# A four-layer graph kernel: the second graph layer's first map made with features on the partitions

## The reference

```python
H = (adj != 0)                       # 1024 x 1024 incidence
w = adj[:, 0, :]                     # first row: weight of each hyperedge
Dn = 1 / einsum('nce,ne->nc', H, w)  # node degree (0 where the sum is 0)
Be = 1 / H.sum(axis=1)               # edge degree
def conv(x, W, b):
    return Dn[:, :, None] * (H @ (Be[:, :, None] * (H.T @ (x @ W.T)))) + b
h = relu(conv(x, W1, b1))            # 256 -> 512 features
h = layer_norm(h, gamma, beta)
y = conv(h, W2, b2)                  # 512 -> 256 features
return y + x
```

## Time and profile before

| | |
|---|---|
| median of 3 runs | 2956.13 us (2955.24 to 2957.43) |
| profiled execution, its own time | 2953.71 us |
| its span, first to last instruction | 2951.9 us |
| PE busy | 2919.8 us (99%) |
| DVE busy | 1871.9 us (63%) |
| ACT busy | 1477.3 us (50%) |
| POOL busy | 719.8 us (24%) |
| mean granted TensorE clock | 0.999 of full speed |

### The profile page before, as it was taken

How to read it: one execution, slowest core, us unless ns; L and a number is a source line. 1 busy time by engine, 2 the same in 40 slices (tenths; PEclk the granted TensorE clock), 3 DMA queues, 4 the chain that set the end, 5 groups by cost and what they waited for, 6 DMA issues and landing times.

```text
span 2951.9 us, 63497 instructions
## 1 busy us (share of the span) xinstructions
PE 2919.8 (99%) x23040; PEld 2374.1 (80%) x23040; DVE 1871.9 (63%) x4154; ACT 1477.3 (50%) x2761; POOL 719.8 (24%) x1305
## 2 busy tenths in 40 slices
PE   8999999999999999999999999999999999999999
PEld 7888788887888878888688886888868888688886
DVE  3797427874288742887428864388643986439862
ACT  2883317833288332883228732387323872238622
POOL 0342003420034201342013420134101341014410
PEclk9999999999999999999999999999999999999999
DMA  5202212023120230211311112112122021220200
GB/s 177 94 2 93 93 58 94 4 92 111 47 87 24 71 135 33 78 51 52 129 51 59 60 59 113 70 40 70 65 97 79 31 86 67 79 79 30 84 8 15
DMA packets 95318, 204.29 MB, mean 69 GB/s; under 512 B 10513, under 2 KB 41617, under 8 KB 94993
## 3 DMA queue, kind: packets, MB, share of 16 engines
q1 hardware_dynamic: 93456, 195.76, 18.3%
q0 software_dynamic: 1536, 4.20, 0.4%
HBM read 136.75 MB, written 8.65 MB: 49 GB/s over the span
## 4 chain that ended last, share of the span: by engine, by line
PE 83%; DVE 12%; ACT 3%; issue 2%; DMA 0%; SPq 0%; DVEq 0%; ACTq 0%
PE ps L1133 39%; PE ps L1319 15%; PE ps L1297 8%; PE ps L1348 8%; PE ps L1410 7%; PE ps L1485 4%; DVE junk L843 3%; DVE stats L640 1%; DVE h L859 1%; DVE dn L852 1%; DVE h L877 1%; PE ps L1173 1%; DVE shiftB L874 1%; ACT Uh L1100 1%; DVE Ul L685 1%
## 5 line engine op out<-in xcount | busy, mean ns | idle before, releaser
L801 DVE CUSTOM_DVE_ANT_0 Z<-ps,adjN 128x1024 f32<-128x1024 f32 x512 | 623.6, 1218 | 54.0 <-PE ps L1297 45.9
L1057 ACT ACTIVATE Z<-Z,nm 128x1024 f32<-128x1024 f32 x512 | 589.7, 1152 | 5.3 <-POOL nm L577 5.3
L1319 PE MATMUL ps<-ident,Z 128*128 128x128 f32 x4096 | 538.5, 274 | 1.4 <-ACT Z L1057 1.2
L1319 PEld LDWEIGHTS ps<-ident,Z 128*128 128x128 f32 x4096 | 463.2, 140 | 88.6 <-issue 38.0
L1297 PE MATMUL ps<-kS,qS 128*128 128x512 f32 x1024 | 371.9, 445 | 3.3 <-issue 2.3
L589 POOL TENSOR_SCALAR H<-adjN 128x128 fp32r<-128x128 f32 (+1 forms) x456 | 317.5, 696 | 0.0
L577 POOL TENSOR_TENSOR nm<-nm,minus 128x1 f32<-128x1 f32 x512 | 97.1, 190 | 550.1 <-DVE nm L801 549.7
L1133 PE MATMUL ps<-mh,adjT 128*128 128x256 f32 x1024 | 223.6, 379 | 0.8 <-issue 0.8
L1133 PE MATMUL ps<-v,P 128*128 128x257 f32 x1024 | 223.6, 379 | 0.0
L1133 PE MATMUL ps<-hT,t3T 128*128 128x512 f32 x512 | 221.0, 592 | 0.0
L1133 PEld LDWEIGHTS ps<-v,P 128*128 128x128 f32 x1024 | 193.8, 189 | 31.9 <-issue 3.8
(11 more groups left out here) (183 smaller groups left out, 5870.8 us busy)
## 6 DMA issues: line engine op xcount, KB each, us to landing
adjT<-adjT_in SPq DMA_DIRECT2D x8, 4096.0 KB, 13.1
adjN<-adj_in SPq DMA_DIRECT2D x8, 4096.0 KB, 17.5
adjT<-adjT_in SPq DMA_DIRECT2D x8, 2048.0 KB, 11.8
qS<-qhi SPq DMA_DIRECT2D x112, 128.0 KB, 2.1
qS<-qlo SPq DMA_DIRECT2D x112, 128.0 KB, 2.1
adjT<-adjT_in SPq DMA_DIRECT2D x8, 1536.0 KB, 6.5
xn<-x_in SPq DMA_DIRECT2D x8, 1024.0 KB, 5.7
out<-x SPq DMA_DIRECT2D x8, 1024.0 KB, 4.9
```

The source lines that it names most:

```text
L801: dve.tensor_tensor_reduce(Z[:, u % ZS], ps[:, 2 * (u % 2):2 * (u % 2) + 2].rearrange("p a n -> p (a n)"), adjN[:, u // HEADS], SCORE_SCAL ...
L1057: act.activation(Z[:, u % ZS], Z[:, u % ZS], ACT.Exp, bias=nm[:, u:u + 1], accum_out=sm[:, u:u + 1]).then_inc(exps.sem, 1)
L1319: mm = pe.transpose(ps[:, turn_bank((u, s)), rows(a)], Z[:, u % ZS, rows(NT // 2 * s + a)], ident[:])
```

## The change

In layer 2:

- **y** is made with features on the partitions: `W1h` is now the stationary side and `A2T` the moving one, in 8 products of 128 features by 512 nodes. The node degree can't be a per-partition scalar there, so it is multiplied into `A2T` by DVE, as a row on all partitions (`dnB`). That row comes from `dn` by two DMAs: out to DRAM in 1024 pieces of 4 bytes (`dn_kept`), and back to all 128 partitions.
- ACT's relu with the bias as a column writes `h2T` at once; the 32 transposes and 8 copies of `h2T` go.
- The row mean is an additional column of ones in `W2g` (products 257 wide). The mean square comes from DVE: four squares and three additions for each half (`add_squares`), which PE sums over the partitions with a column of ones (`sum_squares`). Mean and variance are formed for two node tiles at a time (`moments`), POOL makes `rstd` for these (four times).
- The node weights are computed earlier, two of the eight tiles at steps 66 and 74 of the attention, four before the first `be`, two between; by another instruction (the one that L801 uses), into two `junk` rows. For that `wB` is loaded early.
- `HT`: DVE makes tiles 0 to 4, spread between other work, POOL makes tiles 5 to 7.
- POOL's additions to `x` wait for the inverted node weights.
- **a3** runs in passes: source tiles 0 to 3 for the outputs of the four free banks first, then for the other four.

```diff
-                sp.wait_ge(*adjT_back[2](b, 16))
-                stand(sp, waited_sp)
-                sp.dma_start(wB[:], adj_in[bass.ds(b, 1)][0, 0].partition_broadcast(P)).then_inc(wB_in.sem, 16)
                 sp.dma_start(W1h[:], w1T.rearrange("(t p) d -> p t d", p=P)).then_inc(w2_in.sem, 16)
...
+                sp.wait_ge(*chain(b, 8))
+                stand(sp, waited_sp)
+                sp.dma_start(dn_kept.rearrange("t p -> p t"), dn[:, 3], allow_slow_non_contiguous=True).then_inc(dn_out.sem, 16)
+                sp.wait_ge(*dn_out(b, 16))
+                stand(sp, waited_sp)
+                sp.dma_start(dnB[:], dn_kept.rearrange("t p -> (t p)").partition_broadcast(P)).then_inc(dnB_in.sem, 16)
...
+                for t in range(HT_DVE, NT):
+                    part = [t in tiles for tiles in BACK].index(True)
+                    pool.wait_ge(*adjT_back[part](b, 16))
+                    stand(pool, waited_pool)
+                    pool.tensor_scalar(HT[:, t], adjT[:, t], 0.0, 0.0, ALU.is_equal, ALU.is_equal).then_inc(HTs_pool.sem, 1)
                 pool.wait_ge(*hhs(b, NT))
                 pool.wait_ge(*hls(b, NT))
-                pool.wait_ge(*HTs(b, NT))
+                pool.wait_ge(*chain(b, 8))
                 pool.tensor_tensor(x[:], x[:], hh[:, :, 0:D].bitcast(F32), ALU.add).then_inc(xh.sem, 1)
...
+                for t in range(2, 6):
+                    node_weights(t)
+                incidence_T(0)
+                for t in range(TPH + 1):
+                    edge_degree(t)
                     if t:
                         lower(Ul, Uh, t - 1, uhs, Us)
...
+                incidence_T(1)
+                node_weights(6)
+                incidence_T(2)
+                node_weights(7)
+                invert_weights()
+                for t in range(TPH, NT):
+                    if t - 1 < HT_DVE:
+                        incidence_T(t - 1)
+                    if t + 1 < NT:
+                        edge_degree(t + 1)
+                    lower(Ul, Uh, t, uhs, Us)
+
+                dve.wait_ge(*dnB_in(b, 16))
+                for n in range(DT * NH):
+                    dve.wait_ge(*a2_ps(b, n + 1))
+                    dve.tensor_tensor(A2T[:, n % DT, half(n // DT)], ps[:, 4 + n], dnB[:, half(n // DT)], ALU.mult).then_inc(a2s.sem, 1)
+
+                def add_squares(s):
+
+                    for f in range(FT):
+                        done = (2 * FT - 1) * s + max(0, 2 * f - 1)
+                        dve.wait_ge(*h2Ts(b, FT * s + f + 1))
+                        if f > 1:
+                            dve.wait_ge(*sq_part(b, done))
+                        dve.tensor_tensor(sq[:, s, min(f, 1)], h2T[:, f, half(s)], h2T[:, f, half(s)], ALU.mult).then_inc(sq_part.sem, 1)
+                        if f:
+                            dve.wait_ge(*sq_part(b, done + 1))
+                            dve.tensor_tensor(sq[:, s, 0], sq[:, s, 0], sq[:, s, 1], ALU.add).then_inc(sq_part.sem, 1)
...
+                add_squares(0)
+                add_squares(1)
...
+                mean_squares(0)
+                moments(0)
+                for t in range(0, NT, 2):
+                    if t:
+                        lower_rows(t - 1)
+                    scale_rows(t)
+                    scale_rows(t + 1)
+                    lower_rows(t)
+                    if t == 0:
+                        mean_squares(1)
+                    if t + 2 < NT:
+                        moments(t // 2 + 1)
+                lower_rows(NT - 1)
...
+                for n in range(FT * NH):
+                    s, f = n // FT, n % FT
+                    act.wait_ge(*y_ps(b, n + 1))
+                    act.activation(h2T[:, f, half(s)], ps[:, n % 4], ACT.Relu, bias=b1c[:, f:f + 1]).then_inc(h2Ts.sem, 1)
...
+                sum_squares(0)
...
                 for t in range(NT):
+                    if t == 2:
+                        sum_squares(1)
...
-                sum_up(*of_edges(Uh, Ul, D), (x2s,), [None] * 4 + [x2t(b, t + 1) for t in range(4, NT)], a3_ps)
+                pe.wait_ge(*mean_sq(b, NH))
+                sum_up(*of_edges(Uh, Ul, D), (x2s,), [None] * 4 + [x2t(b, t + 1) for t in range(4, NT)], a3_ps,
+                       passes=((range(TPH), range(TPH)), (range(TPH), range(TPH, NT)), (range(TPH, NT - 2), range(NT))))
```

More of the change, by code:

```diff
@@ L167, in build_program @@
         _, PTb, rs, Rs = p1b
-        h2, h2T = p2
+        _, h2T = p2
         hh, hl, wB, junk = p2a
+        dnB = wB
         Vh, Vl = p2v
         P3, E3 = p3
-        _, shiftB, b1B = p2c
+        _, shiftB = p2c
         (r1, r2, r3) = region(
             [("v", [P, NT, D], F32)],
-            [("W1h", [P, DT, HID], F32), ("W2g", [P, FT, D], F32)],
+            [("W1h", [P, DT, HID], F32), ("W2g", [P, FT, HW], F32)],
             [("xn", [P, NT, D], F32)],
@@ L867, in batch @@
-                for t in range(NT):
-                    if t % TPH == 0:
-                        dve.wait_ge(*nmrs(b, after(3, t // TPH)))
-                    if t == TPH - 1:
-                        shift(b, 3, 1)
+                incidence_T(1)
[9 more added lines that the diff above has]
+                    lower(Ul, Uh, t, uhs, Us)
@@ L1459, in batch @@
-                for t in range(NT):
-                    if t == H2T_AT:
-                        transpose_h2(0)
-                    if t % TPH == 0:
-                        pe.wait_ge(*a2s(b, DT * (t // TPH + 1)))
-                    if t >= 4:
-                        pe.wait_ge(*ys(b, t - 3))
-                    product(ps[:, t % 4], [(A2T[:, c, rows(t)], W1h[:, c]) for c in range(DT)]).then_inc(y_ps.sem, 1)
-                pe.wait_ge(*a2s(b, DT * NH))
-                pe.wait_ge(*w2g_s(b, FT))
@@ L1469, in batch @@
-                for t in range(NT):
-                    if t == TPH - 2:
-                        transpose_h2(1)
-                    if t % TPH == 0:
-                        pe.wait_ge(*h2Ts(b, FT * (t // TPH + 1)))
+                       lambda n, j, i: HT[:, j, half(n // DT)], (incidence_T, Us), [Us(b, n + 1) for n in range(DT * NH)], a2_ps)
+                pe.wait_ge(*w2_in(b, 32))
+                for n in range(FT * NH):
+                    s, f = n // FT, n % FT
+                    if f == 0:
+                        pe.wait_ge(*a2s(b, DT * (s + 1)))
+                    if n >= 4:
+                        pe.wait_ge(*h2Ts(b, n - 3))
+                    product(ps[:, n % 4], [(W1h[:, c, rows(f)], A2T[:, c, half(s)]) for c in range(DT)]).then_inc(y_ps.sem, 1)
@@ new lines, in sum_squares @@
+                def sum_squares(s):
+                    pe.wait_ge(*squares(b, s + 1))
+                    for a in range(TPH):
+                        mm = pe.matmul(ps[:, 4 + s, a:a + 1], sq[:, s, 0, rows(a)], ones[:, 0:1], start=True, stop=True)
+                    mm.then_inc(sq_ps.sem, 1)
+                sum_squares(0)
+                pe.wait_ge(*w2g_s(b, FT))
+                pe.wait_ge(*w2_ones(b, 1))
+                for t in range(NT):
+                    if t == 2:
+                        sum_squares(1)
@@ L1474, in batch @@
                     if t < TPH:
-                        pe.wait_ge(*ys(b, TPH + t + 1))
+                        pe.wait_ge(*h2Ts(b, FT + t + 1))
                     else:
                         pe.wait_ge(*x2t(b, t - 3))
-                    product(ps[:, t % 4, 0:D], [(h2T[:, f, rows(t)], W2g[:, f]) for f in range(FT)]).then_inc(x2_ps.sem, 1)
-                sum_up(*of_edges(Uh, Ul, D), (x2s,), [None] * 4 + [x2t(b, t + 1) for t in range(4, NT)], a3_ps)
+                    product(ps[:, t % 4, 0:D + 1], [(h2T[:, f, rows(t)], W2g[:, f, 0:D + 1]) for f in range(FT)]).then_inc(x2_ps.sem, 1)
```

221 lines of the change are left out of this document (118 added, 103 removed).

## The result

The changed kernel is slower. Its median is 3003.9 us (3001.3 to 3005.5, four runs) against 2955.8 us for the kernel before on the same chip: ratio 1.016, 95% interval 1.015 to 1.017, 48 us. The forecast was 2925 us in a range of 2893 to 2965, so both the sign and the range were wrong.

A forecast was written before the change was run, and what follows sets the result against it. The chain was read as 83% PE and 12% DVE, with DVE nearly always the link before a3's long sum. Terms +3.65 - 4.65 + 0 - 2.85 = -3.85 us per batch, -31 in all: 2956.1 to 2925 us, range 2893 to 2965.

The forecast's parts named there:

- The way to y: Layer 2 up to PE's first y product: y was to start 3.65 us later per batch.
- `HT` 4's hold: DVE's fifth HT pass in a2 waits for POOL's addition x + hh, 3.0 us later per batch.
- The way out: DMA of dn from SBUF to DRAM before y: taken as 4.2 us, 7.4 at the upper end.
- the trip: dn's way to DRAM and back, 4.2 and 4.7 us: dnB at 622.7, before a2's first bank at 623.5.
- The first `be`: DVE's first be pass, after a1's node weights: 1.0 us later, hidden behind PE.
- From y to the first `shiftB`: From PE's start of y to DVE's first shiftB: 14.6 us instead of 19.22, -4.65 per batch.
- First product pair 0.9: Start of y: PE's first two products take 0.9 us, so the first square starts at +1.75.
- its 0.9 x 2 us are not the late ones: PE's x2 products before its third tile, which waits for the second half's squares, do not delay the first shiftB.
- The x2 tiles: The eight x2 tiles, made in pairs 4.25 us apart: 14.75 us against 14.7, priced as 0.
- a3: Products after the last x2 tile: passes leave 90 instead of 114, -2.85 us per batch.
- The lockout by POOL's `HT` passes: Node weights 3, 4 and 5 each wait for one 3.77 us POOL pass: +6.65 us per batch, 3009 us; 12%.
- The DMA rival: dn's way over DRAM is late: at 7.4 us out, y starts 1.1 us later, 2934 us; 17%.

The follow-up runs named there:

- run three: Changed kernel without dn's way over DRAM (A2T multiplied by wB's row), and POOL's additions to x waiting for DVE's five HT passes: 2961.6 us, ratio 1.0014.
- run four: Kernel before with only a3's products made in passes: 2954.1 us, ratio 0.9989.
- run two: Changed kernel with POOL's three additions to x waiting for DVE's five HT passes too: 3031.1 us, ratio 1.025.
- run eight: Changed kernel with all node weights in the attention and all eight HT passes on DVE ahead of be: 2986.5 us, ratio 1.0105.
- run eleven: Changed kernel, POOL's additions waiting for DVE's five HT passes, dn transposed by PE and sent to DRAM as 8 rows: 2962.4 us, ratio 1.0021.
- run one: Changed kernel without dn's way over DRAM, A2T multiplied by the row wB already holds: 2986.8 us, ratio 1.0105.

## Why the prediction was wrong, point by point

- **The way to y**, +3.65 forecast, +7.4 measured. `HT` 4's hold was right: 4.03 us, and 2.5 us of PE's time for the 3.0 of my sum. The way out was taken as 4.2 us and is 8.3; my upper end of 7.4 came from a row of 128 pieces, and the text's own doubt, that 1024 pieces could be slower than any row, was the case. With this the trip, which my sum had hidden, became the later chain. Left out altogether was PE's clock, 1.4 us in six of eight batches. The first `be` came 2.2 us later, measured against a1's end, instead of 1.0; 1.7 us of holds beside POOL's `HT` passes lie ahead of it. With trip and hold gone, run three still needs 2.0 us more than the kernel before: PE waits for DVE's `Ul` and for `HT` 2 and 3, where I had 0.65 for `HT` 3 alone.
- **From y to the first `shiftB`**, -4.65 forecast, +1.2 in the second batch (637.93 to 658.33 against the earlier trace rows). This is the step that failed. "First product pair 0.9", and with it "12.4 for both halves" and "its 0.9 x 2 us are not the late ones", took 24 rows for 24 products; they are 12. A pair with its four rows takes 1.72 us, the squares of both halves ended at +16.2 instead of +12.4, and DVE waited for PE again before the first `moments` (656.31). PE, not DVE, is the bound here, and the two x2 tiles that `moments` needs stand behind all of y.
- **The x2 tiles**, 0 forecast, +0.2 measured; pairs 4.28 us apart, 4.25 forecast. This part held.
- **a3**, -2.85 forecast and -2.82 measured for the last piece, yet worth 0.4 us per batch in run four: the size was right and its worth was not. The products that went ahead of the last x2 tile had been PE work in either place, so moving them gains only where PE idles.
- **Costed at nothing**: the 32 transposes as "PE work beside DVE's". They were the change's one saving of PE work, 3.5 us, and the ones gave 1.6 back. Together the parts behind y give +1.2 + 0.2 - 2.8 = -1.4, the measured y to a4.
- **The rivals.** The lockout by POOL's `HT` passes came near in time (3009), but by chance, as its mechanism was wrong: at most 0.85 us per pass, not 3.77. The Trainium skill's rule (SBUF — State Buffer, "Who interferes with whom"), that the second instruction waits for the whole of the first, holds for POOL's additions (4.03 us on `HT` 4) and not for its one-input passes (of some 4.1 us, beside which DVE's passes lost 0 to 0.85). The DMA rival named the right place and was priced too low, since its upper end was.

The reading at the root was that the chain of waits names the bound. It ran over DVE from 624 to 656, and PE ran beside it, 1.4 us from being the chain itself. A stall in the chain is worth at most the distance to the next chain. The windows cut at PE's marks hinted at that distance (0.7 us), and the rows counted from the code gave it (1.4).

## What to carry to other kernels

Before pricing a gain on the engine that the chain names, sum the work of the other engines between the same two marks; what is left of the interval is the most that the gain can be. Count rows per product, from the code, before taking a duration from a group of rows. And where PE is the bound, judge an edit by what it makes PE wait for as well as by what it saves, since a wait of some microseconds was followed by PE at half its clock.

## What had not been expected of the hardware

- A DMA of 4 KB in 1024 pieces of 4 bytes took 8.2 to 9.8 us from SBUF to DRAM in the changed kernel's eight batches, 9.3 to 11.2 in run two and 9.3 to 12.8 in run eight; one of 8 rows of 512 bytes took 1.3 us in all eight of run eleven (issue to issue of the transfer behind it).
- PE's granted clock fell to 0.5 after it had idled: in six of eight batches after 2.5 us, in three of eight of run one after the same wait, and in all eight of run two after 6.0 to 6.5 us. After the short idle time it came anywhere from 0.4 us before PE resumed to 1.5 us after; in run two it came while PE still idled. What decides between the batches stays open.
- Beside POOL's one-input passes, some of DVE's passes over SBUF took 0.2 to 0.85 us more and others nothing. POOL's took 3.63 to 4.68 us, 4.11 in the mean of 24, where a pass of the same kind and size took 3.77 in the earlier trace rows. That the two stretch each other is a reading of these times, which no run tests.
